# First experts: where TensorE does its side work for the dense layer

## The reference, cut to what matters

```python
x = x + gat(layernorm(x), edge_index, ...)
xn = layernorm(layernorm(x)) * gamma + beta
for e in range(8):                       # first experts
    h = gelu(xn @ W1[e] + b1[e])         # 256 -> 512
    y = y + (h @ W2[e] + b2[e]) * w_full[..., e, None]
x = x + y
x = x + gnn(layernorm(x), ...)           # built as a dense layer from tables
x = x + moe2(layernorm(x), ...)
```

## Time and profile before

| | |
|---|---|
| time, median of 3 runs | 5278.05 us (5275.91 to 5279.58) |
| the profiled execution | 5285.54 us, span 5283.7 us |
| mean granted TensorE clock | 0.847 |
| TensorE busy | 4142.6 us, 78% (weight loads 3005.5 us) |
| VectorE, ScalarE, GpSimd busy | 3392.7, 1671.1, 2168.8 us |
| DMA | 733.83 MB, mean 139 GB/s |

### The profile page before, as it was taken

How to read it: one execution, slowest core, us unless ns; L and a number is a source line. 1 busy time by engine, 2 the same in 40 slices (tenths; PEclk the granted TensorE clock), 3 DMA queues, 4 the chain that set the end, 5 groups by cost and what they waited for, 6 DMA issues and landing times. The chain is left out here.

```text
span 5283.7 us, 86734 instructions
## 1 busy us (share of the span) xinstructions
PE 4142.6 (78%) x27330; PEld 3005.5 (57%) x27331; DVE 3392.7 (64%) x7289; ACT 1671.1 (32%) x2903; POOL 2168.8 (41%) x2194
## 2 busy tenths in 40 slices
PE   3477777777777777746899954899999999769992
PEld 2355555555555555535788843566666666557882
DVE  6366666666666666678555557999999999641115
ACT  1333333333333333313122245433333333222111
POOL 1377777777777777720466620000000000202220
PEclk9677777877787787765999976999999999759996
DMA  4766666666666666644466643445545545323333
GB/s 122 189 171 165 169 168 165 171 162 171 164 169 168 166 171 163 170 115 170 158 199 199 197 149 110 85 91 95 92 87 95 91 88 94 89 81 125 109 111 105
DMA packets 946866, 733.83 MB, mean 139 GB/s; under 512 B 703102, under 2 KB 832054, under 8 KB 944599
## 3 DMA queue, kind: packets, MB, share of 16 engines
q1 hardware_dynamic: 835851, 433.62, 31.8%
q0 software_dynamic: 104144, 289.95, 20.3%
q10 hardware_dynamic: 6652, 7.32, 0.4%
HBM read 483.39 MB, written 92.34 MB: 109 GB/s over the span
## 5 line engine op out<-in xcount | busy, mean ns | idle before, releaser
L1288 POOL DMA_INDIRECT gat_rows<-h_rows,gat_sources x1664 | 1583.5, 952 | 509.6 <-issue 485.9
L1526 PE MATMUL gat_sum_ps<-gat_rows,gat_onehot 128*128 128x265 f32 x3328 | 1167.3, 509 | 3.2 <-DVE gat_rows L1418 2.6
L1526 PEld LDWEIGHTS gat_sum_ps<-gat_rows,gat_onehot 128*128 128x128 f32 x3328 | 792.6, 250 | 190.2 <-issue 5.2
L2062 ACT CAST gnn_z<-build_ps 128x392 bf16<-128x392 f32 x992 | 481.0, 486 | 746.0 <-PE build_ps L2077 745.7
L2086 PE MATMUL back_ps<-zb_pieces,gnn_z 128*128 128x384 bf16 x3038 | 633.5, 325 | 0.0
L2108 PE MATMUL front_ps<-x_res_wide,front_rows 128*128 128x448 bf16 x2604 | 617.8, 351 | 0.0
L2003 DVE TENSOR_TENSOR onehot_low<-dense_codes,dense_iota_bf 128x2048 bf16<-128x2048 bf16 x496 | 603.6, 1217 | 2.1 <-PE build_ps L2077 2.0
L1982 POOL DMA_INDIRECT front_rows<-zf_piece_rows,vrow_nodes x62 | 58.9, 949 | 1145.7 <-PE front_ps L2108 1135.6
L1418 DVE TENSOR_TENSOR gat_rows<-gat_rows,gat_numerators_ps 128x1024 f32<-128x1024 f32 x416 | 502.2, 1207 | 0.0
L2478 PE MATMUL moe_hidden_ps<-moe_rows_T,moe_w 128*128 128x256 f32 (+1 forms) x1408 | 459.5, 482 | 3.0 <-DMA moe_b<-in_L_ffn_b 0.9
L2077 PEld LDWEIGHTS build_ps<-onehot_high,onehot_low 128*128 128x128 bf16 x7936 | 352.3, 98 | 184.2 <-issue 37.3
(11 more groups left out here) (366 smaller groups left out, 5207.8 us busy)
## 6 DMA issues: line engine op xcount, KB each, us to landing
moe_w<-in_L_ffn_W SPq DMA_DIRECT2D x112, 512.0 KB
gat_targets<-gat_step_targets SPq DMA_DIRECT2D x104, 512.0 KB
moe_w<-in_L_ffn_w SPq DMA_DIRECT2D x32, 1024.0 KB
gat_rows<-h_rows,gat_sources POOLq DMA_INDIRECT x1664
moe_rows_out<-moe_slot_zeros SPq DMA_DIRECT2D x36, 512.0 KB
gat_flags<-gat_tile_flags SPq DMA_DIRECT2D x104, 128.0 KB
normal_rows<-moe_xn_all SPq DMA_DIRECT2D x14, 896.0 KB
mid_taken<-moe_rows_out SPq DMA_DIRECT2D x14, 896.0 KB, 7.4
```

What stands on the lines that cost most here:

```text
L1288: pool.indirect_dma_start(out=g[:, b, t, :], out_offset=None, in_=T.h[:, :], in_offset=bass.IndirectOffsetOnAxis(ap=idx[:, b, t:t + 1], ax ...
L1526: last = pe.matmul(po[:, s % BANKS, 0:W], o[:, b, s * SUB + t, :], g[:, b, s * SUB + t, :], start=t == 0, stop=t == SUB - 1)
L2062: nc.scalar.copy(AT[:, k % 2, :, CHUNK * c:CHUNK * (c + 1)], pb[:, c % 2, 0:CHUNK * NT].rearrange("p (u h) -> p h u", u=CHUNK)).then_inc(a ...
```

## The change

TensorE's list of stages in the first experts gets another order: the side stage of group T - 1 is called right behind `hidden` of T - 1, ahead of `turn` of T and `outs` of T - 1. Before, it was called last in the tick. The list of no other engine is changed, nor is the second experts' list.

```diff
             if side is None:
                 staged(pe, groups, [(1, hidden), (0, turn), (1, outs)], 2)
             else:
-                staged(pe, groups, [(1, hidden), (0, turn), (1, outs), (1, side.turn(pe))], 2)
+                staged(pe, groups, [(1, hidden), (1, side.turn(pe)), (0, turn), (1, outs)], 2)
                 side.last(None, pe)
```

## The result

| | before | after |
|---|---|---|
| median | 5277.10 us (4 runs, 5275.91 to 5279.58) | 5238.75 us (4 runs, 5237.48 to 5240.73) |
| ratio | | 0.9927, 95% interval 0.9914 to 0.9939 |
| span of the profiled execution, clock | 5283.7 us, 0.847 | 5237.1 us, 0.848 |
| from the stage's first turn to the next stage's loads | 553.7 us | 517.9 us |

What follows compares the result with a forecast made beforehand. TensorE bounds the stage. Before 506.52 + 4.65 = 511.2 us; after 0.9 + 53 x 9.05 + 5.03 = 485.6; the gain of 25.6 gives 5278 - 26 = 5252 us, range 5243 to 5267.

Steps and rivals of the forecast that it cites:

- The bound: First experts run at TensorE's pace, busy 97.5 us of 100, so only what stands in TensorE's own order counts.
- the sum of the new tick, 9.05: First experts' tick: 3.92 + 0.86 + 0.25 + 0.50 + 3.48 = 9.01 us, plus 0.04, against 9.545 before.
- lower bound of 8.95: First experts' tick in us if the turn's four transposes take less than twice the two code transposes; gain 30.9 us.
- the reserve of 0.04: Us kept per tick for the branch back and TensorE's instructions between four short pieces of work.
- The ends: Stage's start and end: third group starts 0.9 us later (0 to 1.3); the last tick's side work loses 0.38.
- The wait for ScalarE: Ahead of the outputs: the moved work covers the fourth Gelu; starts show 0.80 against 0.50 for the turn.
- The rival that only the visible idle goes: Tick falls only to 9.30, since the branch keeps its gap or instructions can't be fed: 5266 us, chance 0.12.
- The branch: TensorE's loop branch, with 0.3 us of idle loads behind short transposes, is hidden once it follows 16 long output matmuls.
- VectorE and the weights: Both ready in time in the new tick: VectorE with margins of 0.4 us each, weights with 1.0.
- The tick that VectorE alone allows: If VectorE were later, it would set the tick: 4.18 + 0.25 + 0.50 + 3.48 + 0.17 = 8.58 us.
- Both rivals: VectorE or code wait replaces ScalarE's, 5278 us, chance 0.06; weights land late in each tick, 5300 us, chance 0.03.
- The clock: TensorE's clock stays 1.00; rival: it falls with six transposes and sums side by side, about 5319 us, chance 0.02.

Runs made afterwards that it cites:

- only the sums moved: Kernel before with the 32 sums moved between first products and turn, the two code transposes left last: 5253.72 against 5285.73 us, ratio 0.994.
- the side work first: Kernel before with the side work of a group put ahead of the next tick's first products, outputs last: 5278.62 against 5285.73 us, ratio 0.9988.
- the one with the empty instructions: Changed kernel with 48 empty instructions instead of one on SyncE's queue ahead of each weight load: 5240.76 against 5277.43 us for the kernel before.
- the cover alone: Kernel before in its old order, outputs waiting for each chunk's Gelu instead of all four at once: 5260.98 against 5285.73 us, ratio 0.9949.
- the run with VectorE later: Changed kernel with one more 1.2 us one-hot operation on VectorE between a tick's two sets: 5285.22 against 5277.43 us for the kernel before.
- a load 2.1 later: Changed kernel with SyncE's weight load also waiting for the second Gelu of the group before: 5322.63 against 5277.32 us for the kernel before.
- the plain columns: Changed kernel with W1's chunk columns side by side, W2 and b1 reordered to match; b1 turned during routing: 5224.50 against 5277.19 us for the kernel before.

## Why the prediction was right or wrong

**The bound.** Right. The stage goes at TensorE's pace: what its order gains arrives in the time, 53 ticks at 0.725 being 38.4 us, and the stage 35.8 in the execution profiled and 38.3 in that of the changed kernel run again.

**The step that failed: the sum of the new tick, 9.05, with its lower bound of 8.95.** The mechanism held; four terms were too large. The first products were put at 3.92 and took 3.82. That number was read in the tick without a branch, and I took it for the bare work; it held part of a first weight load that stood open behind two short transposes, 0.106 a tick, as the runs with only the sums moved and with the side work first show beside after. The turn was put at 0.50, twice the two codes, and took 0.437: four steps of 0.109, while the codes' 0.25 has one step of 0.143, at the change from sums to codes, that is paid once. The outputs took 3.456 for 3.48, and the reserve of 0.04 was not needed. Together 0.23 a tick, 12.2 us in 53. The lower bound took only the turn for uncertain, so the range ended above the truth; it should have left open how much of the first products was a load that long work hides.

**The ends.** In the stage the 12.2 us more were cut by 2.0. From the first group's first products to the third's took 26.62, 0.98 more than before (forecast 0.9): the loss moved ahead as forecast, with the clock at 0.50 from 2560 to 2565, at the end of the rest units and in the outputs behind them, and the third group's first products at 3.90 instead of 5.35. That the size fits is partly luck: the changed kernel run again has 0.64 more than before, and the one with the empty instructions 2.5. The first products came 1.3 later behind the first turn, for their weights. In the kernels of this study that keep the columns as they were, this takes 1.6 to 4.2 us, without regard to the order. One tick behind the rest units waited for weights, 0.9. The last outputs and the scatter came 0.3 sooner than forecast. By the stage: 25.6 + 12.2 - 1.4 - 0.9 + 0.3 = 35.8. The changed kernel run again has neither loss in full: its first products come 0.2 later than in before and no tick behind the rest units waits, which makes the 38.3. So both belong to the execution profiled and not to the new order. Of before there is one trace alone, so how far its own stage varies isn't shown.

**The wait for ScalarE.** Right that starts show more than idle. The rival that only the visible idle goes fell: the cover alone is worth 24.75 us where the waits showed 10.4.

**The branch.** Right that the outputs hide it; wrong in why it was open. It is the 32 sums close ahead of it, not the two transposes.

**VectorE and the weights.** Right, with margins of 0.33 and 0.84 for the 0.4 and 1.0 forecast. That VectorE's came so close is partly luck, for two misses of 0.1 cancelled: the last one-hot was ready 3.68 behind the outputs' end (2860.50) and not 3.78, and the second half of the sums was due at 4.07 and not 4.18, since the first products are shorter. The tick that VectorE alone allows was put at 8.58 by way of the code; by the second half of the sums, with the same terms, it is 3.78 + 0.43 + 0.25 + 0.50 + 3.48 + 0.17 = 8.61, and the run with VectorE later gives 9.63 - 1.14 = 8.49. The weights were due 0.23 sooner for the shorter tick, and landed about when the forecast had them (7.13 against at most 7.2). Both rivals are real mechanisms with a price now shown, 0.81 a tick for a delay of 1.14 on VectorE and 1.29 for a load 2.1 later; the change left both just short of it. In after the second shows in the steady part nowhere, and near the start at 2586.70; in the changed kernel run again it doesn't show there either.

**The clock.** It is 1.00 in the 100 us of after with six transposes and the sums side by side in each tick. The Trainium skill, "TensorE: Matmul & The Clock Gate", Part 4: PE-mode transpose, says that transposes don't count as activity in the way matmuls do; in this trace joining them cost nothing (1.00).

## What to carry to other kernels

Measure a wait by the starts around it with and without cover, not by the idle that a view of waits shows: here it was worth more than twice that, and a busy share of 97.5 hid 7.6% of a tick. When costing a new order, take each piece's duration from a place where the same kind of work stands ahead of it, since here a first weight load was covered behind long matmuls and stood open behind two short transposes or a wait, and a branch was open behind 32 short sums but not behind the outputs, even with two transposes between. And after such a move name the next margin (here 0.33 us of VectorE, 0.84 of the weights), because the next change will meet it: the plain columns used up nearly all of VectorE's.

## What the runs showed of the hardware that was not expected

A weight load's time depends on how its columns lie: 326 ns for every fourth column, 189 to 190 side by side, for the same 128 columns of f32. The matmuls' step goes with it (0.233 against 0.216), 15 us here. The Trainium skill, "TensorE: Matmul & The Clock Gate", LDWEIGHTS (loading the stationary operand), gives a time by the number of columns alone; the traces differ: besides these two, the 128 columns of bf16 of the sums take 98 ns in after.

Whether a branch on TensorE costs time depends on what is close ahead of it: 0.30 behind 32 sums and two codes (0.31 and 0.44 for the two steps around it against 0.11 and 0.34), 0.25 behind the sums alone, nothing measurable behind the outputs, with or without two transposes between. In the traces it goes with how far ahead of the next first products the branch instruction stands, 0.60 to 0.65 us in the first two cases and 3.56 to 4.49 in the last.

Turning b1 in pieces of 4 bytes cost about 11 us in front of the stage's first loads, 19 beside another stage's loads, and nothing that shows where the DMA engines stood idle.
